# Layer 0's last squares moved to the front of a chunk, layer 2's first step split, and a product ring of four slots

## The reference

```python
e = stack([tbl_f[ids[:, f]] for f in range(39)], axis=1)          # (2048, 39, 16)
x0 = xk = e
for idx, (W, b) in enumerate([(w0, b0), (w1, b1), (w2, b2)]):
    z = relu(einsum('bhd,bkd,hks->bsd', x0, xk, W) + b)            # s = 128
    if idx != 2:  xk, direct = z[:, :64], direct + [z[:, 64:]]
    else:         direct = direct + [z]
h = concatenate([concatenate(direct, axis=1).sum(-1), dense_ctx], axis=1)   # 272
y = relu(relu(h @ W_top1 + b_top1) @ W_top2 + b_top2) @ W_top3
```

## Time and profile before

| | before |
|---|---|
| time, median of 3 runs | 2592.86 us (2591.3 to 2594.6) |
| the profiled execution | 2598.07 us, span 2596.2 us |
| mean granted TensorE clock | 0.984 |
| busy: PE, DVE, POOL, ACT | 94%, 84%, 72%, 64% of the span |
| DMA | 136 GB/s over the span, 347 MB by SP's queue |

### The profile page before, as it was taken

How to read it: one execution, slowest core, us unless ns; L and a number is a source line. 1 busy time by engine, 2 the same in 40 slices (tenths; PEclk the granted TensorE clock), 3 DMA queues, 4 the chain that set the end, 5 groups by cost and what they waited for, 6 DMA issues and landing times.

```text
span 2596.2 us, 32413 instructions
## 1 busy us (share of the span) xinstructions
PE 2443.5 (94%) x8654; PEld 1591.3 (61%) x8654; DVE 2169.6 (84%) x1872; ACT 1661.3 (64%) x2120; POOL 1875.1 (72%) x1270
## 2 busy tenths in 40 slices
PE   0899999999999999999999999999999999999989
PEld 0466666666656666666666666666666666666655
DVE  1588889889878888988988898898888888888880
ACT  1566666666666666766666676666666666666653
POOL 6578778777867777777787777778777777765450
PEclk6899999999999999999999999999999999999999
DMA  2677667667757766766776676677667666756730
GB/s 71 139 149 155 126 138 166 134 131 151 154 110 152 154 130 132 166 137 132 148 158 129 132 164 140 127 150 155 131 131 166 141 131 145 160 129 129 159 80 0
DMA packets 214715, 352.58 MB, mean 136 GB/s; under 512 B 34382, under 2 KB 47566, under 8 KB 214588
## 3 DMA queue, kind: packets, MB, share of 16 engines
q1 hardware_dynamic: 194717, 347.07, 61.6%
q0 software_dynamic: 19968, 5.15, 2.2%
HBM read 346.97 MB, written 5.12 MB: 136 GB/s over the span
## 4 chain that ended last, share of the span: by engine, by line
POOL 30%; issue 27%; PE 16%; DVE 9%; DMA 7%; ACT 7%; SPq 3%; POOLq 0%; ACTq 0%; DVEq 0%; another core or an unknown queue 0%
POOL emb L374 13%; POOL Pl L380 13%; DMA xb<-x_dram 7%; ACT Ph L514 5%; PE ps L807 5%; PE ps L797 4%; DVE P L692 3%; DVE ps L692 3%; PE ps L817 3%; POOL dir L404 3%; SPq L311 3%; DVE Pl L697 3%; PE ps L926 1%; PE ps L918 1%; POOL emb L385 1%
## 5 line engine op out<-in xcount | busy, mean ns | idle before, releaser
L380 POOL TENSOR_TENSOR Pl<-P,Ph 128x1024 fp32r<-128x1024 f32 x448 | 1072.3, 2397 | 479.1 <-ACT Ph L514 469.4
L692 DVE TENSOR_TENSOR P<-xb,ps 128x1024 f32<-128x1024 f32 x768 | 926.8, 1214 | 81.1 <-DMA xb<-x_dram 72.9
L807 PE MATMUL ps<-Ph,wh 128*128 128x512 f32 x1920 | 870.1, 459 | 8.1 <-ACT Ph L514 8.0
L697 DVE TENSOR_TENSOR Pl<-ps,Ph 128x1024 fp32r<-128x1024 f32 x512 | 626.1, 1223 | 178.9 <-ACT Ph L514 168.7
L374 POOL DMA_INDIRECT emb<-tbl_in,idx x624 | 601.0, 963 | 166.3 <-issue 145.3
L807 PE MATMUL ps<-Ph,wl 128*128 128x512 f32 x1792 | 707.4, 395 | 0.0
L514 ACT ACTIVATE Ph<-ps 128x1024 fp32r<-128x1024 f32 x512 | 523.3, 1022 | 285.3 <-DVE ps L692 217.3
L817 PE MATMUL ps<-Pl,wh 128*128 128x512 f32 x1920 | 689.7, 445 | 11.4 <-POOL Pl L380 11.3
L514 ACT ACTIVATE Ph<-P 128x1024 fp32r<-128x1024 f32 x448 | 474.6, 1059 | 325.3 <-DVE P L692 303.8
L692 DVE TENSOR_TENSOR ps<-xb,ps 128x1024 f32<-128x1024 f32 x512 | 628.2, 1227 | 28.1 <-DMA xb<-x_dram 10.2
L797 PE MATMUL ps<-P,wp 128*128 128x512 f32 x1280 | 603.7, 594 | 4.1 <-DVE P L692 4.1
(11 more groups left out here) (64 smaller groups left out, 826.7 us busy)
## 6 DMA issues: line engine op xcount, KB each, us to landing
xb<-x_dram SPq DMA_DIRECT2D x1280, 256.0 KB, 8.5
emb<-tbl_in,idx POOLq DMA_INDIRECT x624
x_dram<-rows_sb SPq DMA_DIRECT2D x64, 78.0 KB
xb<-w_in SPq DMA_DIRECT2D x15, 128.0 KB
xb<-wt_in SPq DMA_DIRECT2D x2, 512.0 KB, 8.6
xb<-dense_in SPq DMA_DIRECT2D x1, 768.0 KB, 5.9
wp<-w_in SPq DMA_DIRECT2D x5, 128.0 KB
xb<-w0a_in SPq DMA_DIRECT2D x1, 448.0 KB
```

Source lines behind the costliest of these rows:

```text
L380: pool.tensor_tensor(Pl[:, h_slot(ref, c, k)], P[:, p_slot(ref, c, k)], Ph[:, h_slot(ref, c, k)], ALU.subtract).then_inc(low_pool, 1)
L692: dve.tensor_tensor(p, xb[:, x], xk.unsqueeze(1).broadcast_to([128, 2, N]), ALU.mult)\
L697: dve.tensor_tensor(Pl[:, h_slot(ref, c, k)], p_ps, Ph[:, h_slot(ref, c, k)], ALU.subtract)\
L807: pe.matmul(z_of(c, k), w[:, q, j, :], Ph[:, h_slot(ref, c, k), j, :], start=k in (L1B, L2) and i + j == 0, stop=False)
```

## The change

Step 10 (layer 2's first) goes from P to V: its product is written to `p_ps`, ScalarE rounds it, VectorE subtracts, and TensorE runs six fp32r matmuls in place of four plain passes. There are then 16 split steps per chunk, and both `Ph` and `Pl` have four slots. The rest of layer 0 is the first of the seven sums: its sum is at step 2, its squares at step 5 (`rest_squares`), `rest_low` comes after product 6 on VectorE in the same chunk, and it is contracted at step 9. The other six sums stand at steps 5 to 15, their contractions at 8 to 18. Each of them still waits for `aux_read`, so the second sum (step 5) waits for `rest_low`. `direct0`, `upper` and `lower` of layer 0 move to steps 0, 1 and 2. The gathers are spread over the tile by hand in `GATHERS`, the next ids are taken at step 18 of chunk 1, the second activation on the embeddings moves from step 15 to 17, and layer 2's relu from step 5 to 4. The MLP's dense input has a buffer of its own.

```diff
-KIND = "GVPVGPVGVPPGVGVGVPVG"
+KIND = "GVPVGPVGVPVGVGVGVPVG"
-PRING, HRING = 4, 5
+PRING, HRING = 4, 4
-SUM_AT = [3, 5, 7, 9, 11, 13, 15]
-SQUARE_AT = [6, 7, 10, 12, 14, 16, 18]
-CONTRACT_AT = [6, 8, 10, 12, 14, 16, 19]
-REST_AT = 1
-DIRECT0_AT, UPPER0_AT, LOWER0_AT, RELU2_AT, DIRECT1_AT, RELU1_AT = 2, 3, 4, 5, 7, 8
-HIGH_AT, FULL_AT, LOW_AT = 15, 15, 17
+SUM_AT = [2, 5, 7, 9, 11, 13, 15]
+SQUARE_AT = [5, 7, 10, 12, 14, 16, 18]
+CONTRACT_AT = [9, 8, 10, 12, 14, 16, 18]
+REST_AT = 6
+DIRECT0_AT, UPPER0_AT, LOWER0_AT, RELU2_AT, DIRECT1_AT, RELU1_AT = 0, 1, 2, 4, 7, 8
+HIGH_AT, FULL_AT, LOW_AT = 15, 17, 17
-GATHER_AT = [k for k in range(STEPS) if KIND[k] != "G"]
+NEXT_IDS_AT = (1, 18)
+GATHERS = [[1, 2, 3, 5, 9, 14, 16, 17, 18], [1, 2, 3, 5, 6, 8, 9, 10, 18, 18],
+           [1, 2, 3, 5, 6, 9, 10, 12, 14, 16, 17], [1, 2, 3, 5, 6, 8, 9, 10, 17]]
...
+        dense0 = sb("dense0", [DX, 2 * N], F32R)
-        FREED = (0, 2, 3, 4)
+        FREED = (0, 1, 2, 3)
-        dense = (Ph[0:DX, (all_splits + 1) % HRING].rearrange("p a n -> p (a n)"), sel0[0:DX, :])
+        dense = (dense0[:, :], sel0[0:DX, :])
-            early = 12
+            early = 13
...
+            def rest_squares(T, number):
+                act.wait_ge(aux_ready, T * PER["aux"] + number + 1)
+                act.activation(sqx[:, :], aux_ps[0:REST0], ACT.Square).then_inc(rest_high, 1)
+                act.wait_ge(rest_high, T * CPT + number // AUX + 1)
+                act.activation(aux_ps[LAST_LO], aux_ps[LAST_LO], ACT.Square).then_inc(rest_square, 1)
...
-            rest_low(0, 1)
...
+                if s == 1:
+                    rest_low(0, 1)
...
-                        if k == REST_AT and not end and not (first and c == 0):
-                            rest_low(T, c + 1)
+                        if k == REST_AT and not (last and c >= 2):
+                            rest_low(T, c + 2)
...
-                rows = R0 if t < FULL0 else REST0
+                rows, t = (R0, t - 1) if t else (REST0, FULL0)
...
-            def contract0(t, bank):
-                if t < FULL0:
-                    pe.matmul(z0_ps[:, bank], w0[:, t, :], sq[:, t % 2, :], start=t == 0, stop=False)
+            def contract0(t, bank, start, stop):
+                if t:
+                    m = pe.matmul(z0_ps[:, bank], w0[:, t - 1, :], sq[:, (t - 1) % 2, :], start=start, stop=stop)
                 else:
-                    pe.matmul(z0_ps[:, bank], w0x[:, :], sqx[:, :], start=False, stop=True).then_inc(squares_done, 1)
+                    m = pe.matmul(z0_ps[:, bank], w0x[:, :], sqx[:, :], start=start, stop=stop)
```

More of the change, by code:

```diff
@@ L431, in tile @@
             def tile(T, ref, fields, first=False, last=False):
+                todo = [list(f) for f in fields]
                 for c in range(CPT):
[L434 to L437, removed]
                     for k in range(STEPS):
@@ L440, in tile @@
                             low(T, ref, c, k)
[L441 to L445, removed]
+                        if (c, k) == NEXT_IDS_AT and todo[2]:
+                            next_ids(T + 2)
+                        part = min(c, 1) if (c, k) < NEXT_IDS_AT else 2
+                        n = GATHERS[c].count(k) * (1 + (first and c == 0))
+                        for f in todo[part][:n]:
+                            gather(f)
+                        todo[part] = todo[part][n:]
                         if c == 0 and not first and k in FOLD1_AT:
@@ L463, in tile @@
                             low_emb(T + 1)
-            cuts = (0, 12, 21, 30, NF)
-            third, fourth, first, second = (range(a, b) for a, b in zip(cuts, cuts[1:]))
-            tile(0, 0, (range(early, 30), range(30, NF), third, fourth), first=True)
+            late, soon = len(GATHERS[0]), len([k for k in GATHERS[1] if (1, k) < NEXT_IDS_AT])
+            cut = NF - late - soon
+            assert sum(map(len, GATHERS)) == NF
+            start, middle, rest = range(0, cut), range(cut, cut + late), range(cut + late, NF)
+            tile(0, 0, (range(early, cut + late), rest, start), first=True)
             with pool.Fori(1, TILES - 2) as T:
-                tile(T, 1, (first, second, third, fourth))
-            tile(TILES - 2, TILES - 2, (first, second, (), ()))
-            tile(TILES - 1, TILES - 1, ((), (), (), ()), last=True)
+                tile(T, 1, (middle, rest, start))
+            tile(TILES - 2, TILES - 2, (middle, rest, ()))
+            tile(TILES - 1, TILES - 1, ((), (), ()), last=True)
             pool.wait_ge(z2_read, chunks)
@@ L500, in square @@
                 act.wait_ge(aux_ready, T * PER["aux"] + number + 1)
-                if t < FULL0:
[L502 to L506, removed]
+                act.activation(sq[:, t % 2, :], aux_ps, ACT.Square).then_inc(aux_read, 1)
+            def rest_squares(T, number):
[3 more added lines that the diff above has]
+                act.activation(aux_ps[LAST_LO], aux_ps[LAST_LO], ACT.Square).then_inc(rest_square, 1)
             def round_(T, ref, c, k):
@@ L537, in _ @@
                 copy_x(0, AUX * g)
-                for t in range(T0):
-                    square(0, AUX * g + 1 + t, t)
+                rest_squares(0, AUX * g + 1)
+                for t in range(1, T0):
+                    square(0, AUX * g + 1 + t, t - 1)
                     s = t - (T0 - PRE - 1)
@@ L574, in tile @@
                             t = SQUARE_AT.index(k)
-                            square(T, aux + 1 + t, t)
+                            if t:
+                                square(T, aux + 1 + t, t - 1)
+                            else:
+                                rest_squares(T, aux + 1)
                         if c == 1 and not last:
@@ L609, in tile @@
                             act.wait_ge(dense_in, 16)
-                            act.wait_ge(split_done, dense_left)
                             for i in range(2):
@@ L779, in sums @@
             def sums(t):
-                rows = R0 if t < FULL0 else REST0
+                rows, t = (R0, t - 1) if t else (REST0, FULL0)
                 pe.matmul(aux_ps[0:rows], sel[:, t, 0:rows], x2[:, :], start=True, stop=True)\
                     .then_inc(aux_ready, 1)
-            def contract0(t, bank):
-                if t < FULL0:
-                    pe.matmul(z0_ps[:, bank], w0[:, t, :], sq[:, t % 2, :], start=t == 0, stop=False)
-                else:
-                    pe.matmul(z0_ps[:, bank], w0x[:, :], sqx[:, :], start=False, stop=True).then_inc(squares_done, 1)
+            def contract0(t, bank, start, stop):
+                if t:
+                    m = pe.matmul(z0_ps[:, bank], w0[:, t - 1, :], sq[:, (t - 1) % 2, :], start=start, stop=stop)
+                else:
+                    m = pe.matmul(z0_ps[:, bank], w0x[:, :], sqx[:, :], start=start, stop=stop)
+                if stop:
+                    m.then_inc(squares_done, 1)
             def z_of(c, k):
@@ L860, in _ @@
                     if t:
-                        contract0(t - 1, g)
+                        contract0(t - 1, g, t == 1, False)
                     if g and t >= T0 - PRE:
@@ L864, in _ @@
                 pe.wait_ge(aux_read, AUX * (g + 1))
-                contract0(T0 - 1, g)
+                contract0(T0 - 1, g, False, True)
             assert not late
@@ L880, in tile @@
                         if k in CONTRACT_AT and not no0:
-                            t = CONTRACT_AT.index(k)
-                            if t == 0:
+                            t, opens = CONTRACT_AT.index(k), k == min(CONTRACT_AT)
+                            if opens:
                                 pe.wait_ge(products, upto(T, ref, STEP, c, L1B - 1))
                             pe.wait_ge(aux_read, aux + 2 + t)
-                            contract0(t, c % 2)
+                            contract0(t, c % 2, opens, t == T0 - 1)
                         if k in SUM_AT and not no0:
```

1 line of the change is left out of this document (removed).

## The result

The changed kernel takes 2673.12 us (median of 4, 2667.84 to 2675.49), the kernel before 2592.26 in the same comparison: a ratio of 1.0308, 95% interval 1.029 to 1.0326. The forecast had the direction and a period made of the right pieces, but 2636 us, and the result lies above its range (2660). One execution of a_both_late, and one of the kernel before beside it, were slow at a lower granted clock (0.80 and 0.76), and the ratios leave them out.

What follows compares the result with a forecast made beforehand. The prediction took a ring through product 10, the x transfers, product 5, TensorE, ACT and low 8 as the bound: 38.6 us a chunk against 37.92, +43 us over 62 chunks, 2636 us by the median; range 2588 to 2660.

Steps and rivals of the forecast that it cites:

- TensorE's 0.32 us on step 10: Six fp32r matmuls replacing four plain passes save TensorE 0.32 us a chunk; off the ring, so worth 0.
- its stop at step 19: TensorE's wait for the rest's low part at the contraction, 1.3 us a chunk, removed by putting the rest first.
- The ring is: product 10, transfers, product 5, TensorE, ACT, low 8: Closed path taken to bound the kernel before; its edges sum to 37.95 us, a whole period.
- The 38.6 us: Forecast period per chunk of the changed kernel, 1.26 + 1.26 + 26.2 + 3.4 + 2.39 + 4.10, against 37.92.
- 26.2: Time in us from SP's first issue of the 20 spread DMAs to product 5 of the next chunk.
- 3.4 us: From product 5 to plain 5, with the second sum waiting for `rest_low`; 2.87 seen before, +0.53 on the ring.
- I take 0, because product 3 and product 4 wait for landings anyway: Moving `direct0` to `lower` to steps 0 to 2 can hold low 1 by up to 0.68 us; counted as 0.
- the start, the last two chunks and the MLP I take as they are, within 4 us: Parts outside the steady chunks were assumed unchanged, within 4 us.
- 0 for the ring of four: Rounds wait for the split four back, one less; taken as 0, bounds 0 and 0.4 us.
- 0 for the gathers: A gather ahead of a low on GpSimd can delay it about 1 us; taken as 0, upper bound 0.4.
- TensorE comes late by itself: Rival: TensorE reaches step 5 late, `rest_low` is hidden, its own work bounds; -1.1 us a chunk, 2525 us; chance 0.12.
- DVE closes the ring: Rival: landings come earlier, DVE's 27.8 us from low 8 to product 5 holds; 2580 to 2611 us; chance 0.12.

Runs made afterwards that it cites:

- a_both_late: Changed kernel with the second sum moved behind plain 5 and `direct0`, `upper`, `lower` back at ScalarE's steps 2 to 4: 2608.34 us, 1.0036 of the kernel before.
- a_sum_behind: Changed kernel with the second sum moved from step 5 to 6, behind plain 5 and low 4: 2622.44 us, 1.0102 of the kernel before.
- a_direct0_late_half: Changed kernel with `direct0`, `upper`, `lower` at steps 2 to 4 and every load of x cut to half its columns: 2590.5 us, 0.9968 of the kernel before.
- b_rest0: Kernel before with `rest_low` after product 0 of the next chunk in place of product 1: 2556.78 us, 0.985 of the kernel before.
- b_split10: Kernel before with step 10 split and rings of four slots, rest and sums where they were: 2691.21 us, 1.0373 of the kernel before.
- b_ring4: Kernel before with `Ph` and `Pl` of four slots in place of five and the dense input in its own buffer: 2596.63 us, 0.9991.
- a_half: Changed kernel with only the loads of x cut to half their columns: 2653.46 us, 1.0209 of the kernel before.
- a_direct0_late: Changed kernel with `direct0`, `upper` and `lower` of layer 0 back at ScalarE's steps 2, 3 and 4: 2672.19 us, 1.029 of the kernel before.

## Why the prediction was wrong

**The direction held, and for the changed kernel the mechanism.** TensorE's 0.32 us on step 10 was worth nothing, its stop at step 19 was not lost time won but a wait that moved to the second sum, and the ring of product 10, transfers, product 5, `rest_low`, plain 5, `direct1` and low 8 closes the changed kernel's period. a_sum_behind and a_direct0_late_half each cut one edge of it and the time followed, in a_sum_behind by half. Product 10 came at 1.26 as taken, `direct1` to low 8 at 4.10.

**"The ring is: product 10, transfers, product 5, TensorE, ACT, low 8" was wrong for the kernel before.** The sum of 37.95 us was no evidence for it: starts added up round any closed path give the period. In the earlier trace rows TensorE runs without a gap from the rest's contraction (1246.14) to plain 5 (1255.76), and product 5 (1252.89 and 1.21 us long) had been done for 1.7 us. The tight path goes from low 8 through VectorE to `rest_low` (20.92 us in the mean), through TensorE to plain 5 (10.37), to `direct1` (2.52) and to low 8 (4.10), 37.91 in all. The runs bear this out: with `rest_low` one product earlier the period fell 0.61 us (b_rest0), and with a split on VectorE's way to it b_split10 took 2691 us, where the transfers' ring would give 2600. The 38.6 us sums the changed kernel's ring, which does bind, so it does not rest on this; but that the ring I had wrongly read in the kernel before became the binding one is luck.

**The step that failed in the sum is "26.2", from first issue to product 5: it was mis-sized.** It measured 26.52 in the mean. I had read it from one chunk; the mean of the kernel before was already 26.29. Another 0.2 is between the two traces: the last loads land 26.2 us after the first issue, against 25.9 before (means of the landings). But b_ring4, no slower than the kernel before, also has 26.44 and 26.2, so this 0.2 is not shown to come from the split or the new order. Why the same 20 transfers take longer I can't say; nothing was tried on it. 0.3 x 62 = 19 us. In the windows of after the full engines moved 215 to 227 GB/s. The fit in the Trainium skill ("DMA: Bandwidth & Descriptors", section "Anatomy of one DMA"), 2.0 us plus bytes at 436 GB/s, is for DMAs that GpSimd issues, which the prediction does not say; here SP issues the loads. By that fit, as an estimate, the loads would be out of the ring; these rows and the gain of a_direct0_late_half speak against that rate here.

**"3.4 us" for the lag** measured 3.47, 4 us in all.

**For `direct0` to `lower` at steps 0 to 2, "I take 0, because product 3 and product 4 wait for landings anyway"** was right in its result and wrong as a reason for calm. In the cycle shown it holds low 1 by 1.03 us, over the upper bound of 0.68 I gave it, since it is not one activation but the wait for TensorE's step 18 that stands in front of rounds 0 and 1. Its ring is 38.74 (a_half) beside the transfers' 39.01, so it costs little now, but it eats what any repair of the others would bring: 0.69 of 1.51 us in a_sum_behind.

**"the start, the last two chunks and the MLP I take as they are, within 4 us"**: they gave 7.5 us. By the sum: forecast +43 on the profiled execution; with 19, 4 and 7.5 it is 74, and the span grew by 75.5. The medians lie another 5 us apart.

**0 for the ring of four and 0 for the gathers** held: b_ring4 0.9991, and with the old gathers 5 us more.

**The rival "TensorE comes late by itself"** is refuted: TensorE waited at the second sum in 63 chunks. "DVE closes the ring" holds only where the transfers are halved; with the loads whole, the transfers bind. The range was too narrow because it took the bounds of single edges and no error for edges that I had read off one chunk.

## What to carry to other kernels

When several engines go round in one ring, a wait that is removed comes back at the next place where the same data is late, and what counts is the sum of the edges and not the size of the wait. That a path's edges add up to the period proves nothing, since every closed path does that: ask of each edge whether its end waited for its start. Take each edge as a mean over many chunks, since 0.3 us of 26 was half of the miss here. Two rings of nearly equal length hide each other: an edit that shows nothing alone (a_direct0_late) can be worth 14 us beside another, so test in pairs before calling a place free. And look for the small operation that closes the ring: moving 0.7 us of work by one step (b_rest0) brought 1.5%, more than any of the larger rearrangements.

## What the runs showed of the hardware

In b_split10 the granted clock fell again and again inside the loop, its mean was 0.978 where b_ring4 had 0.994. Windows of b_split10 (columns as in the earlier trace rows), and the timeline of PE at the same place:

```profile
1001.00:1011.00 10.00, 8.21 (x31) 5.33 (x29) 9.81 (x9) 5.89 (x8) 6.98 (x5) 1.00 1.08 214
1011.20:1014.60 3.40, 3.25 (x8) 2.57 (x9) 3.30 (x4) 1.85 (x3) 2.95 (x3) 0.51 1.07 223
1014.60:1024.00 9.40, 9.40 (x39) 6.58 (x37) 7.82 (x8) 6.41 (x9) 5.91 (x5) 1.00 0.34 68
```

```profile
1011.36 0.79 PE L788 MATMUL ps<-sqx,w0x 76*128 76x512 f32 x1 [2.14 <-DVE sqx L702]
```

TensorE had stood 2.14 us at the rest's contraction; in the next window the clock was 0.51, the lower level of 1.2 GHz, and then full again. Of chunks 4 to 59, leaving out chunk 16, 22 had such a fall; they took 40.1 to 40.3 us each. The other 33 took 38.6 to 39.1, with a median of 38.6 (21.75 from low 8 to `rest_low`, 10.37 to plain 5, 2.39 and 4.10). That is 22 x 1.6 = 35 us, more than a third of the 95 us over b_ring4. All 22 had stood 2.13 to 2.17 us at the contraction. But 17 other chunks had stood 2.13 us or more as well and kept the full clock, so a stop of that length does not decide it alone. In the changed kernel the stops for `rest_low` were 1.2 us in the mean and 2.0 at most (72.8 us in 62 waits of the matmul), and from chunk 2 to the end of the loop the clock stayed at full speed. That the stops are the reason is not shown: it is read from the order of events, and no run varied them alone.
